# High and low halves of the first two expert layers' inputs as one moving operand of 512

## The reference, cut to what matters

```python
logits = jnp.einsum('bsd,de->bse', x, Wg) + bg
probs = jax.nn.softmax(logits, axis=-2)
vals, idx = jax.lax.top_k(jnp.transpose(probs, (0, 2, 1)), 128)
tok = x[bidx, idx]                                             # 2 batches, 16 experts, 128 tokens, 512
h = jax.nn.relu(jnp.einsum('bekd,edo->beko', tok, w1) + b1b)   # layer 0: 512 -> 512
h = jax.nn.relu(jnp.einsum('bekd,edo->beko', h, w2) + b2b)     # layer 1: 512 -> 512
h = jnp.einsum('bekd,edo->beko', h, w3) + b3b                  # layer 2: 512 -> 512
outputs = jnp.zeros((B, S, O), x.dtype).at[bidx, idx].add(h * vals[..., None])
```

## Time and profile before

| | |
|---|---|
| median of 3 runs | 756.65 us (756.55 to 757.57) |
| span of the profiled execution | 754.2 us (the page gives its span; its time with what lies around the span is not listed apart) |
| PE busy | 703.4 us, 93% |
| DVE busy | 559.2 us, 74% |
| ACT busy | 397.7 us, 53% |
| POOL busy | 432.6 us, 57% |

### The profile page before, as it was taken

How to read it: one execution, slowest core, us unless ns; L and a number is a source line. 1 busy time by engine, 2 the same in 40 slices (tenths; PEclk the granted TensorE clock), 3 DMA queues, 4 the chain that set the end, 5 groups by cost and what they waited for, 6 DMA issues and landing times.

```text
span 754.2 us, 12492 instructions
## 1 busy us (share of the span) xinstructions
PE 703.4 (93%) x4420; PEld 622.3 (83%) x4420; DVE 559.2 (74%) x994; ACT 397.7 (53%) x616; POOL 432.6 (57%) x602
## 2 busy tenths in 40 slices
PE   6999999999999999999997059999999999999995
PEld 5766888888888888888896048999999999999994
DVE  5776789888898988886877993666666666666661
ACT  5755355454444445345763303666666666666641
POOL 2825788888888888777784704244443333333223
PEclk9999999999999999999999569999999999999999
DMA  8600122221222221110124615388888887778744
GB/s 316 249 29 14 43 84 76 82 71 56 100 72 74 82 82 62 56 59 29 59 85 146 240 47 168 123 235 245 236 235 233 240 240 233 237 243 230 204 85 56
DMA packets 53902, 102.89 MB, mean 136 GB/s; under 512 B 5392, under 2 KB 6480, under 8 KB 53840
## 3 DMA queue, kind: packets, MB, share of 16 engines
q1 hardware_dynamic: 46672, 85.31, 34.0%
q0 software_dynamic: 7168, 16.78, 9.9%
HBM read 76.68 MB, written 25.17 MB: 135 GB/s over the span
## 4 chain that ended last, share of the span: by engine, by line
PE 51%; DMA 20%; issue 17%; DVE 8%; POOL 2%; ACT 1%; POOLq 0%; DVEq 0%; ACTq 0%
PE bank L261 26%; DMA out<-y,ids 19%; PE bank L268 6%; PE banks L638 4%; PE banks L644 4%; PE banks L261 2%; PE banks L648 2%; PE banks L649 2%; DVE pack L1736 1%; DVE left L1746 1%; DVE pos L1738 1%; PE bank L702 1%; PE bank L755 0%; PE banks L770 0%; DMA tok<-xn,ids 0%
## 5 line engine op out<-in xcount | busy, mean ns | idle before, releaser
L2113 POOL DMA_INDIRECT out<-y,ids x32 | 76.2, 2380 | 171.1 <-DVE y L1905 166.2
L1402 DVE TENSOR_TENSOR w_l<-w_raw,w_h 128x2048 fp32r<-128x2048 f32 x45 | 103.0, 2290 | 31.5 <-ACT w_h L1075 31.5
L1353 ACT ACTIVATE h<-bank,b 128x512 f32<-128x512 f32 x64 | 44.0, 687 | 106.0 <-PE bank L261 102.8
L1402 DVE TENSOR_TENSOR hT_l<-h,hT_h 128x512 fp32r<-128x512 f32 x64 | 44.2, 691 | 65.3 <-ACT hT_h L1359 65.3
L1075 ACT ACTIVATE w_h<-w_raw 128x2048 fp32r<-128x2048 f32 x48 | 90.6, 1925 | 2.2 <-DMA w_raw<-w 2.2
L1390 DVE BATCH_NORM_STATS2 bn<-x 128x6 f32<-128x512 f32 x113 | 77.7, 688 | 8.3 <-DMA x<-x 5.5
L261 PE MATMUL bank<-tokT_h,w_l 128*128 128x256 f32 x252 | 71.3, 283 | 0.0
L261 PE MATMUL bank<-tokT_h,w_h 128*128 128x256 f32 x252 | 71.3, 283 | 0.0
L261 PE MATMUL bank<-tokT_l,w_h 128*128 128x256 f32 x252 | 71.3, 283 | 0.0
L261 PE MATMUL bank<-hT_h,w_l 128*128 128x256 f32 x240 | 67.9, 283 | 0.0
L261 PE MATMUL bank<-hT_l,w_h 128*128 128x256 f32 x240 | 67.9, 283 | 0.0
(11 more groups left out here) (320 smaller groups left out, 2249.2 us busy)
## 6 DMA issues: line engine op xcount, KB each, us to landing
w_raw<-w SPq DMA_DIRECT2D x48, 1024.0 KB, 6.4
x<-x SPq DMA_DIRECT2D x32, 256.0 KB, 2.7
out<-x SPq DMA_DIRECT2D x32, 256.0 KB, 2.2
xn<-xn SPq DMA_DIRECT2D x32, 256.0 KB, 2.0
mask<-mask_t SPq DMA_DIRECT2D x8, 256.0 KB, 3.4
stage<-wk SPq DMA_DIRECT2D x1, 1024.0 KB, 7.8
stage<-wq SPq DMA_DIRECT2D x2, 512.0 KB, 7.8
stage<-wf SPq DMA_DIRECT2D x1, 1024.0 KB, 10.2
```

The lines of the kernel that those rows point to most:

```text
L1353: act.activation(h32[n % 2][:, :], ps_hid[n % 4][:, :], ACT.Relu, bias=bias)
L1402: dve.tensor_tensor(dst, src, hi_part, ALU.subtract).then_inc(sem, 1)
L2113: pool.indirect_dma_start(out=out_rows, out_offset=bass.IndirectOffsetOnAxis(ap=ids[:, r:r + 1], axis=0), in_=y[e % 2][b][:, :], in_offset ...
```

## The change

The tiles of an input's high and low parts become one tile, 512 columns wide, high in columns 0 to 255 and low in 256 to 511. One matmul of 512 columns multiplies the weights' high part with both; one of 256 columns adds the weights' low part times the input's high part to the first 256 columns. An output chunk now fills a bank of its own, with high x high + low x high in its first half and high x low in its second. The four banks hold four chunks instead of four pairs, and PE waits for `d_pre` of four chunks earlier before it reuses one.

The halves are added when the bank is emptied. ACT copies the second half, with the bias, into `cross`. DVE adds the first half, from the bank, to `cross`, into `pre`, and raises `d_pre`. ACT takes the relu of `pre` into `h_h`. DVE computes max(`pre`, 0) - `h_h` into `h_l` in one instruction. The chunk counts in other waits are doubled accordingly.

```diff
-    tok_h, tok_l = place("tokT_h", [P, C, B * P], F32R), place("tokT_l", [P, C, B * P], F32R)
-    h32 = [place(f"h32_{i}", [P, 2 * B * P]) for i in range(2)]
-    h_h = [place(f"hT_h{i}", [P, C, B * P], F32R) for i in range(2)]
-    h_l = [place(f"hT_l{i}", [P, C, B * P], F32R) for i in range(2)]
+    BOTH = B * P
+    tok_x = place("tokT", [P, C, 2 * BOTH], F32R)
+    tok_h, tok_l = tok_x[:, :, 0:BOTH], tok_x[:, :, BOTH:]
+    pre = [place(f"h_pre{i}", [P, 2, BOTH]) for i in range(2)]
+    cross = [place(f"h_cross{i}", [P, BOTH]) for i in range(4)]
+    h_x = [place(f"hT{i}", [P, C, 2 * BOTH], F32R) for i in range(2)]
+    h_h, h_l = [t[:, :, 0:BOTH] for t in h_x], [t[:, :, BOTH:] for t in h_x]
...
+        def chunk(bank, wh, wl, x, c, parts):
+
+            f = slice(c * P, (c + 1) * P)
+            for d in parts:
+                pe.matmul(bank[:, :], wh[:, d, f], x[:, d, :], start=(d == 0), stop=False)
+                last = pe.matmul(bank[:, 0:BOTH], wl[:, d, f], x[:, d, 0:BOTH], start=False, stop=(d == C - 1))
+            return last
+
         def hidden(e, layer):
...
+            for c in range(C):
+                n = 8 * e + 4 * layer + c
                 if n >= 4:
-                    pe.wait_ge(sm.a_h, n - 3)
...
+                    pe.wait_ge(sm.d_pre, n - 3)
...
+                    last = chunk(ps_hid[n % 4], wh, wl, x, c, range(C))
                 last.then_inc(sm.p_h, 1)
...
             pe.wait_ge(sm.d_hlo, 1)
-            some(0, (0, 1))
-            some(2, (0, 1))
+            pe.wait_ge(sm.d_pre, 1)
+            chunk(ps_hid[0], wh, wl, x, 0, (0, 1))
+            pe.wait_ge(sm.d_pre, 2)
+            chunk(ps_hid[1], wh, wl, x, 1, (0, 1))
             pe.wait_ge(sm.d_hlo, 2)
...
         def relu(e, layer, pair):
             n = 4 * e + 2 * layer + pair
-            act.wait_ge(sm.p_h, n + 1)
-            if n >= 2:
-                act.wait_ge(sm.d_hlo, n - 1)
-            bias = (b1, b2)[layer][:, e:e + 1]
-            act.activation(h32[n % 2][:, :], ps_hid[n % 4][:, :], ACT.Relu, bias=bias)
+            for o in range(2):
+                m = 2 * n + o
+                act.wait_ge(sm.p_h, m + 1)
+                act.wait_ge(sm.d_pre, max(0, m - 3))
+                act.activation(cross[m % 4][:, :], ps_hid[m % 4][:, BOTH:], ACT.Identity,
+                               bias=(b1, b2)[layer][:, e:e + 1]).then_inc(sm.a_cross, 1)
+            act.wait_ge(sm.d_pre, 2 * n + 2)
...
-            src = ps_hid[n % 4][:, :].rearrange("p (a t) -> p a t", a=2)
-            act.activation(h_h[layer][:, 2 * pair:2 * pair + 2, :], src, ACT.Relu, bias=bias).then_inc(sm.a_h, 1)
+            act.activation(h_h[layer][:, 2 * pair:2 * pair + 2, :], pre[n % 2][:, :, :], ACT.Relu)\
+                .then_inc(sm.a_h, 1)
...
         def hidden_lo(e, layer, pair):
             n = 4 * e + 2 * layer + pair
+            if n >= 2:
+                dve.wait_ge(sm.d_hlo, n - 1)
+            for o in range(2):
+                m = 2 * n + o
+                dve.wait_ge(sm.a_cross, m + 1)
+                dve.tensor_tensor(pre[n % 2][:, o, :], ps_hid[m % 4][:, 0:BOTH], cross[m % 4][:, :], ALU.add)\
+                    .then_inc(sm.d_pre, 1)
             dve.wait_ge(sm.a_h, n + 1)
-            src = h32[n % 2][:, :].rearrange("p (a t) -> p a t", a=2)
             part = slice(2 * pair, 2 * pair + 2)
-            lo(sm.d_hlo, h_l[layer][:, part, :], src, h_h[layer][:, part, :])
+            dve.scalar_tensor_tensor(h_l[layer][:, part, :], pre[n % 2][:, :, :], 0.0, h_h[layer][:, part, :],
+                                     ALU.max, ALU.subtract).then_inc(sm.d_hlo, 1)
```

More of the change, by code:

```diff
@@ L72, in build @@
         g_r1 g_r2 g_r3 g_r4 g_b4 g_x1b g_xd g_qlo g_x2b s_lo
-        g_zero c_bcol k_full k_max k_top k_cand k_got k_half k_moved k_ids k_sum k_exp k_tr k_out k_pos a_soft
+        d_pre a_cross g_zero c_bcol k_full k_max k_top k_cand k_got k_half k_moved k_ids k_sum k_exp k_tr k_out k_pos a_soft
         a_w d_w g_w p_tok a_thi d_tlo a_h d_hlo p_h p_y d_y
@@ L438, in used @@
         else:
-            eng.wait_ge(sm.p_h, 4 * e + 2 * layer + 2)
+            eng.wait_ge(sm.p_h, 8 * e + 4 * layer + 4)
     block = ctx.enter_context(nc.Block())
@@ L953, in hidden @@
                 pe.wait_ge(sm.d_tlo, 2 if e == 0 else B * (e + 1) + 1)
-                xh, xl = tok_h, tok_l
+                x = tok_x
             else:
                 pe.wait_ge(sm.d_hlo, 4 * e + 2)
-                xh, xl = h_h[0], h_l[0]
-            for pair in range(2):
-                n = 4 * e + 2 * layer + pair
+                x = h_x[0]
+            for c in range(C):
+                n = 8 * e + 4 * layer + c
                 if n >= 4:
-                    pe.wait_ge(sm.a_h, n - 3)
[L962 to L975, removed]
+                    pe.wait_ge(sm.d_pre, n - 3)
+                if (e, layer, c) == (0, 0, 0):
+                    chunk(ps_hid[n % 4], wh, wl, x, c, (0, 1))
+                    pe.wait_ge(sm.d_tlo, 3)
+                    last = chunk(ps_hid[n % 4], wh, wl, x, c, (2, 3))
+                else:
+                    last = chunk(ps_hid[n % 4], wh, wl, x, c, range(C))
                 last.then_inc(sm.p_h, 1)
@@ L980, in first_second_layer @@
             wh, wl = weights(when[(0, 1)])
[L981 to L991, removed]
+            x = h_x[0]
             pe.wait_ge(sm.d_hlo, 1)
-            some(0, (0, 1))
-            some(2, (0, 1))
+            pe.wait_ge(sm.d_pre, 1)
+            chunk(ps_hid[0], wh, wl, x, 0, (0, 1))
+            pe.wait_ge(sm.d_pre, 2)
+            chunk(ps_hid[1], wh, wl, x, 1, (0, 1))
             pe.wait_ge(sm.d_hlo, 2)
[L997 to L1000, removed]
+            chunk(ps_hid[0], wh, wl, x, 0, (2, 3)).then_inc(sm.p_h, 1)
+            chunk(ps_hid[1], wh, wl, x, 1, (2, 3)).then_inc(sm.p_h, 1)
+            pe.wait_ge(sm.d_pre, 4)
+            chunk(ps_hid[2], wh, wl, x, 2, range(C)).then_inc(sm.p_h, 1)
+            chunk(ps_hid[3], wh, wl, x, 3, range(C)).then_inc(sm.p_h, 1)
         def outputs(e):
@@ L1342, in token_hi @@
                 act.wait_ge(sm.p_tok, B * e + b + 1)
-                act.wait_ge(sm.p_h, max(0, 4 * (e - 1) + 2))
+                act.wait_ge(sm.p_h, max(0, 8 * (e - 1) + 4))
                 for part in token_parts(e, b):
@@ L1348, in relu @@
             n = 4 * e + 2 * layer + pair
-            act.wait_ge(sm.p_h, n + 1)
-            if n >= 2:
-                act.wait_ge(sm.d_hlo, n - 1)
-            bias = (b1, b2)[layer][:, e:e + 1]
-            act.activation(h32[n % 2][:, :], ps_hid[n % 4][:, :], ACT.Relu, bias=bias)
+            for o in range(2):
[5 more added lines that the diff above has]
+            act.wait_ge(sm.d_pre, 2 * n + 2)
             if layer == 0:
-                act.wait_ge(sm.p_h, 4 * e)
+                act.wait_ge(sm.p_h, 8 * e)
             else:
                 act.wait_ge(sm.p_y, B * e)
-            src = ps_hid[n % 4][:, :].rearrange("p (a t) -> p a t", a=2)
-            act.activation(h_h[layer][:, 2 * pair:2 * pair + 2, :], src, ACT.Relu, bias=bias).then_inc(sm.a_h, 1)
+            act.activation(h_h[layer][:, 2 * pair:2 * pair + 2, :], pre[n % 2][:, :, :], ACT.Relu)\
+                .then_inc(sm.a_h, 1)
         token_hi(0)
```

## The result

The changed kernel takes 782.13 us (median of 4 runs, 781.92 to 782.48); the kernel before 756.69. The ratio is 1.0333, with a 95% interval of 1.0318 to 1.0348: 3.3% slower. Forecast were 783.0 us and a range of 772 to 802.

The account below looks back on a forecast made before the run. PE bounded the kernel at 17.85 us per expert; the change would close a DVE-ACT loop of 19.72 us. 14 x 1.87 = +26.2, expert 0 +0.1, so 756.65 + 26.3 = 783.0 us, range 772 to 802.

Parts of the forecast that it names:

- The loop: Expert stage: one expert's round through DVE's and ACT's queues takes 19.72 us, where PE's was 17.85; 14 times, +26.2 us.
- pair, first add to next pair: DVE, emptying a pair of banks: from its first add to the next instruction after its subtract, 2.09 us.
- first add to subtract: DVE, within a pair: two adds, then standing still for ACT's relu; the subtract starts 1.45 us after the first add.
- subtract to split_lo B: DVE, from layer 0's last subtract to the expert's second split, with token_lo twice and ACT's split in between: 2.78 us.
- last subtract to split_lo A: DVE, from layer 1's last subtract to the next expert's first split, behind ACT's split: 1.80 us.
- DVE subtract (scalar_tensor_tensor): DVE's subtract at the end of each pair: 0.722 us long, where it was 0.69.
- PE no longer last, its idle in one piece at the bank wait: PE idles 2.3 us per expert, in one piece ahead of layer 0, released by DVE's first layer-1 add.
- Launch and end: Outside the span and what is changed: the median of the runs is 2.45 us above the 754.2 us span.
- PE's own gain: Hidden-layer matmuls: 0.360 becomes 0.347 us, 0.43 less per expert, 6.9 over 16 experts, not seen as PE isn't last.
- rival A: Expert stage: each pair's hand-over is hidden and PE stays last; 6.9 us faster, 749.8 us. Chance 0.07.
- Expert 0 and the tail: Ahead of the loop only the longer last pair shows, +0.1 us; behind expert 15's first split nothing more.
- Rival B: PE's idle drops its clock to 1.2 GHz, layer 0 needs 5.55 us more; 828 us. Chance 0.09.

Follow-up runs that it names:

- e4: Changed kernel, per layer ACT makes four crosses then two relus and DVE four adds then two subtracts: 753.91 us, ratio 0.9961 to the kernel before.
- e1: Changed kernel, but ACT's relu reads the crosses it wrote itself, not DVE's sums; result not the reference's: 753.35 us, ratio 0.9955 to before.
- e5: Changed kernel with only DVE reordered (four adds, then two subtracts per layer), ACT's order kept: 777.27 us, ratio 1.0273 to before.
- e3: Changed kernel with one more 128x256 DVE add per pair, ahead of the pair's first add: 802.39 us, ratio 1.0602 to before.
- e7: e4 with PE doing a chunk's four 512-column matmuls, then its four of 256, not in turns: 752.88 us, ratio 0.9949 to the kernel before.

## Why the prediction was right

*The loop.* Right in place and nearly in size. Forecast 19.72 us per expert, measured 19.65; forecast 14 periods of +1.87 = 26.2, measured 25.21. That the two spans differ by 26.1, so near the 26.3 of the forecast, is partly luck: the loop came out 1.0 lower, expert 0 0.46 higher than forecast, and another 0.46 arose ahead of the loop. The medians, 25.4 apart, are the fairer comparison, 0.9 below the forecast. The single terms:

| term | forecast | measured |
|---|---|---|
| pair, first add to next pair | 2.09 | 2.06 |
| first add to subtract | 1.45 | 1.45 |
| subtract to split_lo B | 2.78 | 2.77 |
| last subtract to split_lo A | 1.80 | 1.81 |
| DVE add | 0.42 | 0.416 |
| ACT cross | 0.470 | 0.465 |
| ACT relu from SBUF | 0.622 | 0.632 |
| DVE subtract (scalar_tensor_tensor) | 0.722 | 0.693 |

The subtract is the one price off by more than 0.01: I took the mean of two rows of 0.682 and 0.762 as it stood, and the operation costs what the tensor_tensor did. That is the 0.03 in the pair.

*PE no longer last, its idle in one piece at the bank wait.* Right: 14 waits, all there. The size was off: forecast 2.3 us per expert, measured 19.65 - 17.62 = 2.0 (1.8 as the profile counts idle, from a matmul's end).

*Launch and end.* The 2.45 us that I took for what lies around the span compared a median with the span of another, shorter execution; where a run lists both, it is 1.8 (782.11 and 780.3). The forecast adds to the median, so nothing hangs on it.

*PE's own gain.* Mis-sized: 0.43 us per expert forecast, from 0.360 - 0.347 per chunk (the same rows, 11.51 - 32 x 0.347, give 0.41); measured 17.85 - 17.62 = 0.23 (e4), as a pair costs 0.352 and not 0.227 + 0.120. It was hidden in the changed kernel, so it cost the forecast nothing, but rival A's 749.8 us was 3.5 us too low: e1, which is rival A made real, has 753.35. The row was from `outputs`, the same width in another place; of the 6.9 us that I thought the change could bring at best, half was there.

The rule that I had set beside it, the 2.5 ns above N/2.4 of the Trainium skill ("TensorE: Matmul & The Clock Gate", Back-to-back issue gap), is further off: 512 and 256 columns together are 325 ns by it, an estimate, and the trace has 352 to 354. That section gives the rule for single matmuls and other figures for a stream with a weight load before each, which this kernel has; but its 131 ns for 512 columns in such a stream isn't borne out either, as the trace has 227.

*Expert 0 and the tail.* Forecast +0.1 and nothing; measured +0.56 and -0.31. In expert 0 DVE waits for the second cross in three of the four pairs (0.25, 0.20 and 0.62 us), ahead of the stop for the relu; I had counted only its last pair. How the 0.56 divides among them was not tried.

*Rival B, the clock.* The fall happened, against my "The clock stays 1.00", and cost nothing. Windows of two periods (columns as in rows 2), and PE at a place where the clock fell:

```profile
614.45:634.10 19.65, 17.78 (x89) 15.06 (x88) 14.85 (x19) 11.82 (x18) 7.00 (x5) 0.91 0.71 213
634.10:653.76 19.66, 19.36 (x107) 16.52 (x106) 14.86 (x19) 12.05 (x18) 7.02 (x5) 1.00 0.75 214
```

```profile
548.73 0.28 PE L956 MATMUL bank<-hT,w_l 128*128 128x256 f32 x1
550.79 0.66 PE L955 MATMUL bank<-tokT,w_h 128*128 128x512 f32 x1 [1.78 <-DVE h_pre L1897]
...
551.46 0.63 PE L955 MATMUL bank<-tokT,w_h 128*128 128x512 f32 x1
```

PE ends at 549.01, stands idle 1.78 us, and starts at the 1.2 GHz level: the next pair takes 551.46 - 550.79 = 0.67 in place of 0.354. By 554.39 the pairs start 0.35 apart again. The clock fell like this after three of the ten idles of 1.78 to 1.88 us (the first window above, with a mean of 0.91, has another), and not after the seven others. In e5, with no idle above 1.55, it is 1.00 all the way from 480 to 740 us; in e3 it fell after five of eight idles of about 2.7. My comparison with the busy share of two stretches told none of this. The period stays 19.65 or 19.66 with it or without: PE lost 1.6 us or so, and had 2.0 to give. Rival B had priced it at 5.55, as if all of layer 0 ran at half clock. In e4, where PE does not idle, the clock is 1.00. The Trainium skill's warning ("TensorE: Matmul & The Clock Gate", A second HAM failure mode) of a clock that swings with short idles between groups bears on this kernel after all, as far as the clock goes; in the time it was not to be seen.

## What to carry to other kernels

A change that saves issues on the last engine and gives the emptying of its banks one more hand-over has to be priced as a loop through the queues: write down the start of each instruction on the emptying engine over one period, in its order, with every round trip, and compare the sum with the period of the engine that is last. Load did not tell this one (14.9 of 19.65 us); the sum of the starts did, to 0.4%. When such a loop is closed by round trips, issue all first halves before the second halves, on both engines: here that turned 3.3% slower into 0.4% faster without one instruction less.

## What the runs showed of the hardware that I had not expected

- PE's clock went to 1.2 GHz after three idles of 1.78 to 1.88 us and stayed at 2.4 GHz after seven others as long; it cost the kernel nothing, since PE had 2.0 us to give per expert. A matmul pair of 512 and 256 columns took 0.64 to 0.67 us there, 0.354 at the full clock.
- A 512-column matmul takes 0.227 us from its start to the next in `outputs` and 0.232 on average in the two hidden layers (e7), same width and type.
- A hand-over between ACT and DVE costs 0.03 to 0.04 us, in both directions: the 0.70 of a stop is nearly all the relu itself.
